# First attention of a four-part block on one core: TensorE turns x itself, the norm enters as scalars of the rows, and GpSimd splits one weight pair

## The reference, cut to what matters

```python
x = x + tanh(g_xattn[0]) * xattn0(layernorm(x), ctx)   # energy = (ctx Wq + bq)(ctx Wk + bk)^T; softmax; LN(x) @ att^T
x = x + tanh(g_ffn[0])   * ffn0(layernorm(x))          # ternary weights, rows rounded to 8 bits, SiLU gate
x = x + tanh(g_xattn[1]) * xattn1(layernorm(x), ctx)   # 16 heads, q and k RMS-normed, softmax, Wo
x = x + tanh(g_ffn[1])   * moe(layernorm(x))           # 64 experts, top 8, and a shared one
```

## Time and profile before

| | |
|---|---|
| time, median of 3 runs | 615.57 us (615.5 to 616.37) |
| span of the profiled execution | 614.4 us |
| TensorE busy | 604.4 us (98%) |
| VectorE busy | 477.4 us (78%) |
| ScalarE busy | 422.5 us (69%) |
| GpSimd busy | 235.1 us (38%) |

### The profile page before, as it was taken

The page is one execution under the profiler, slowest core; times in us unless marked ns, Lnnn a source line. Parts: engine busy times, 40 slices in busy tenths (PEclk is TensorE's granted clock), DMA queues, the critical chain, the costliest instruction groups (busy, mean ns, idle before and its releaser), DMA issues.

```text
span 614.4 us, 11617 instructions
## 1 busy us (share of the span) xinstructions
PE 604.4 (98%) x3644; PEld 525.1 (85%) x3644; DVE 477.4 (78%) x1139; ACT 422.5 (69%) x1082; POOL 235.1 (38%) x280
## 2 busy tenths in 40 slices
PE   8989999999999999999999999999999999999997
PEld 6757899999999999999998888888887888887886
DVE  3999988887777787688876787788777676777776
ACT  6999999888888888889897344465444444443442
POOL 5899998576665566656662020000000000000000
PEclk9999999999999999999999999999999999999999
DMA  8513302000000000000030544353856466555640
GB/s 294 201 53 102 92 13 78 2 2 2 2 1 2 1 2 2 1 2 1 11 121 2 169 150 152 128 171 97 215 156 167 116 174 175 153 158 152 188 133 34
DMA packets 33653, 56.47 MB, mean 92 GB/s; under 512 B 12800, under 2 KB 13504, under 8 KB 33600
## 3 DMA queue, kind: packets, MB, share of 16 engines
q1 hardware_dynamic: 33312, 55.82, 30.5%
q10 hardware_dynamic: 288, 0.00, 0.0%
HBM read 53.45 MB, written 1.31 MB: 89 GB/s over the span
## 4 chain that ended last, share of the span: by engine, by line
PE 87%; DVE 5%; ACT 3%; POOL 2%; issue 2%; DVEq 0%; POOLq 0%; ACTq 0%
PE bank L299 25%; PE bank L301 24%; PE bank L300 24%; PE bank L968 4%; PE bank L943 2%; PE bank L935 2%; DVE hs L2072 1%; PE bank L895 1%; PE bank L1009 1%; PE bank L815 1%; PE bank L821 1%; PE bank L888 1%; ACT w L1461 1%; PE bank L801 1%; POOL att L585 1%
## 5 line engine op out<-in xcount | busy, mean ns | idle before, releaser
L1607 ACT ACTIVATE inter_hi<-inter 128x512 fp32r<-128x512 f32 x63 | 39.8, 632 | 140.6 <-DVE inter L2271 140.6
L299 PE MATMUL bank<-xnT_hi,front_hi 128*128 128x512 f32 (+1 forms) x260 | 102.0, 392 | 0.0
L301 PE MATMUL bank<-xnT_hi,front_lo 128*128 128x512 f32 (+1 forms) x260 | 101.7, 391 | 0.0
L300 PE MATMUL bank<-xnT_lo,front_hi 128*128 128x512 f32 (+1 forms) x260 | 101.7, 391 | 0.0
L2275 DVE TENSOR_TENSOR inter_lo<-inter,inter_hi 128x512 fp32r<-128x512 f32 x63 | 43.6, 692 | 37.9 <-ACT inter_hi L1607 37.3
L1559 ACT ACTIVATE att<-bank,shift,rq 128x256 f32<-128x256 f32 x128 | 71.2, 572 | 0.0
L585 POOL TENSOR_TENSOR att<-att,rowinv 128x512 f32<-128x512 f32 x60 | 63.1, 1067 | 11.7 <-DVE rowinv L2171 11.7
L2244 DVE TENSOR_TENSOR prod<-gate_s,bank 128x512 f32<-128x512 f32 x63 | 43.2, 686 | 21.7 <-PE bank L301 19.6
L2154 DVE TENSOR_REDUCE rowmax<-bank 128x2 f32<-128x512 f32 x64 | 43.6, 685 | 21.0 <-PE bank L301 20.7
L300 PEld LDWEIGHTS bank<-xnT_lo,front_hi 128*128 128x128 f32 x260 | 48.9, 188 | 11.3
L301 PEld LDWEIGHTS bank<-xnT_hi,front_lo 128*128 128x128 f32 x260 | 48.8, 188 | 11.3
(11 more groups left out here) (271 smaller groups left out, 1813.1 us busy)
## 6 DMA issues: line engine op xcount, KB each, us to landing
w_all<-w_rows SPq DMA_DIRECT2D x128, 128.0 KB, 3.0
raw<-in_expert_w SPq DMA_DIRECT2D x32, 384.0 KB, 3.5
wvo_raw<-in_expert_w SPq DMA_DIRECT2D x16, 384.0 KB, 3.6
e_more<-in_expert_w SPq DMA_DIRECT2D x16, 384.0 KB, 3.6
raw<-in_head_qk SPq DMA_DIRECT2D x8, 384.0 KB, 3.2
wvo_raw<-in_head_vo SPq DMA_DIRECT2D x4, 384.0 KB, 3.8
w_keep<-in_head_vo SPq DMA_DIRECT2D x4, 384.0 KB, 3.6
gate_raw<-in_gate_wT SPq DMA_DIRECT2D x2, 704.0 KB, 8.8
```

The source lines that it names most:

```text
L299: pe.matmul(out, l_hi, r_hi_, start=start, stop=False, skip_group_check=True)
L300: pe.matmul(out, l_hi, r_lo_, start=False, stop=False, skip_group_check=True)
L301: return pe.matmul(out, l_lo, r_hi_, start=False, stop=stop, skip_group_check=True)
L1607: act.activation(inter_hi[:, slot, :], inter[:, slot, :], ACT.Copy).then_inc(a_Ihi, 1)
```

## The change

- The rows are no longer normed ahead of the first attention. `normalise_0` goes (eight calls), and `turn_rows_0` turns x as soon as it is loaded. Two of its calls stand earlier in TensorE's order, and one copy earlier in ScalarE's.
- `power_0` makes two more columns: `tg_rstd`, gate times r, and `tg_mean`, gate times r times m. `add_A` uses `tg_rstd` as its factor, one instruction for each tile. `tg_mean` is taken off in `add_output`, after the second attention, again one instruction for each tile.
- Pair 0's two parts are made by GpSimd (`both_w(0)`); `split_w(0)` and `low_w(0)` go. SP's wait for `load_qk(2)` and the counts of the other waits follow; `split_done(p)` on TensorE waits for `g_Wlo` at p = 0.

```diff
+        tg_rstd = sb("tg_rstd", [P, TILES])
+        tg_mean = sb("tg_mean", [P, TILES])
...
@@ SP's queue @@
             load_vo(2)
+            sp.wait_ge(g_Wlo, 1)
+            load_qk(2)
             sp.wait_ge(v_Wlo, 1)
-            load_qk(2)
-            sp.wait_ge(v_Wlo, 2)
             load_qk(3)
...
@@ GpSimd @@
+            def pool_high_w(p):
+
+                pool.wait_ge(l_hqk[p % 2], (p // 2) * 16 + 16)
+                pool.tensor_scalar(w_hi(p), raw[:, p % 2, :], 1.0, 0.0, ALU.mult, ALU.add).then_inc(g_Whi, 1)
+
+            def pool_low_w(p):
+                pool.wait_ge(g_Whi, 1 if p == 0 else 2)
+                pool.tensor_tensor(w_lo(p), raw[:, p % 2, :], f(w_hi(p)), ALU.subtract).then_inc(g_Wlo, 1)
+
             def both_w(p):
...
+                pool_high_w(p)
+                pool_low_w(p)
...
             def root_0(b):
                 c = slice(2 * b, 2 * b + 2)
                 pool.wait_ge(v_pw1, b + 1)
-                pool.tensor_scalar(negm[:, c], mv[:, c, 0], -1.0, 0.0, ALU.mult, ALU.add)
                 pool.tensor_scalar(vare[:, c], mv[:, c, 1], 1.0, EPS, ALU.mult, ALU.add).then_inc(g_va0, 1)
 
             def power_0(b):
...
-                pool.tensor_tensor(rstd[:, c], vare[:, c], minus_half[:, 0:2], ALU.pow).then_inc(g_pw1, 1)
+                link_g(pool, pool.tensor_tensor(rstd[:, c], vare[:, c], minus_half[:, 0:2], ALU.pow))
+                if b == 0:
+                    pool.wait_ge(a_tg, 1)
+                link_g(pool, pool.tensor_scalar(tg_rstd[:, c], rstd[:, c], tg[:, 0:1], 0.0, ALU.mult, ALU.add))
+                pool.tensor_tensor(tg_mean[:, c], mv[:, c, 0], tg_rstd[:, c], ALU.mult).then_inc(g_pw1, 1)
...
             root_0(0)
             power_0(0)
-            normalise_0(0)
-            normalise_0(1)
             root_0(1)
             power_0(1)
-            normalise_0(2)
-            normalise_0(3)
+            scale_gain(g1, l_g1)
             root_0(2)
             power_0(2)
-            normalise_0(4)
-            normalise_0(5)
-            scale_gain(g1, l_g1)
             root_0(3)
...
             scale_back_1(0)
             limit_1(0)
-            normalise_0(6)
+            both_w(0)
             scale_back_1(1)
+            limit_1(1)
             scale_gain(g2, l_g2)
-            normalise_0(7)
-            limit_1(1)
             times_gain(0)
...
@@ TensorE @@
             def turn_rows_0(b, bk):
 
-                pe.wait_ge(g_u0, 2 * b + 2)
+                pe.wait_ge(l_x[b // 2], 16)
                 for k in range(KH):
                     for t in range(2):
                         mm = pe.transpose(bank4(bk)[:, k, t * P:(t + 1) * P],
-                                          u[:, 2 * b + t, k * P:(k + 1) * P], ident[:, :])
+                                          x[:, 2 * b + t, k * P:(k + 1) * P], ident[:, :])
                 mm.then_inc(t_u0, 1)
...
             query_key(0, 2, 3)
             energy(0, 2)
+            turn_rows_0(0, 1)
             query_key(1, 2, 0)
             energy(1, 6)
             energy(2, 0)
-            turn_rows_0(0, 1)
             pe.wait_ge(a_eA, 4)
             turn_att(0, 6)
             energy(3, 3)
             mix(0, 1)
+            turn_rows_0(1, 5)
             turn_att(1, 2)
-            turn_rows_0(1, 5)
             sum_abs([0, 1], 0)
...
@@ ScalarE @@
             copy_qk(0, 2, 4, 3)
+            copy_rows_0(0, 1)
             copy_qk(1, 2, 5, 0)
             exp_A(0, 2)
             exp_A(1, 6)
-            copy_rows_0(0, 1)
...
             abs_down()
-            split_w(0)
             turn_gate(0)
...
@@ VectorE @@
             def add_A(b, bk):
                 dve.wait_ge(t_oA, b + 1)
-                if b == 0:
-                    dve.wait_ge(a_tg, 1)
-                xb = x[:, 2 * b:2 * b + 2, :]
-                dve.scalar_tensor_tensor(xb, bank4(bk), tg[:, 0:1], xb, ALU.mult, ALU.add).then_inc(v_xA, 1)
+                dve.wait_ge(g_pw1, b + 1)
+                for t in range(2):
+                    i = 2 * b + t
+                    ins = dve.scalar_tensor_tensor(x[:, i, :], bank4(bk)[:, t, :], tg_rstd[:, i:i + 1], x[:, i, :],
+                                                   ALU.mult, ALU.add)
+                ins.then_inc(v_xA, 1)
...
             def add_output(b):
 
                 dve.wait_ge(t_Y, 16 * b + 16)
-                xb = x[:, 2 * b:2 * b + 2, :]
-                dve.tensor_tensor(xb, bank4(YBK), xb, ALU.add).then_inc(v_Y, 1)
+                for t in range(2):
+                    i = 2 * b + t
+                    ins = dve.scalar_tensor_tensor(x[:, i, :], bank4(YBK)[:, t, :], tg_mean[:, i:i + 1], x[:, i, :],
+                                                   ALU.subtract, ALU.add)
+                ins.then_inc(v_Y, 1)
...
             absmax_1(1)
-            low_w(0)
             inv_max_1(1)
```

More of the change, by code:

```diff
@@ L159, in flamingo_kernel @@
         g_gain, v_sc1, v_sc2, g_sc1, g_sc2 = (sem(n) for n in ("g_gain", "v_sc1", "v_sc2", "g_sc1", "g_sc2"))
-        g_u0, t_u0, a_x0 = sem("g_u0"), sem("t_u0"), sem("a_x0")
+        t_u0, a_x0 = sem("t_u0"), sem("a_x0")
         g_u1, v_u, t_u, a_u, c_u = sem("g_u1"), sem("v_u"), sem("t_u"), sem("a_u"), sem("c_u")
@@ L237, in flamingo_kernel @@
                              "v_mq", "v_Olo", "v_Mlo", "v_gk"))
-        g_rk, g_rq, g_kn, g_att, v_Wlo, g_Wlo = (sem(n) for n in ("g_rk", "g_rq", "g_kn", "g_att", "v_Wlo", "g_Wlo"))
+        g_rk, g_rq, g_kn, g_att, v_Wlo, g_Wlo, g_Whi = (sem(n) for n in ("g_rk", "g_rq", "g_kn", "g_att", "v_Wlo", "g_Wlo",
+                                                                  "g_Whi"))
         dctx = ExitStack()
@@ L339, in _ @@
             load_vo(4)
-            sp.wait_ge(v_Wlo, 3)
+            sp.wait_ge(v_Wlo, 2)
             load_qk(4)
@@ L344, in _ @@
             load_vo(7)
+            sp.wait_ge(v_Wlo, 3)
+            load_qk(5)
             sp.wait_ge(v_Wlo, 4)
-            load_qk(5)
-            sp.wait_ge(v_Wlo, 5)
             load_qk(6)
-            sp.wait_ge(g_Wlo, 1)
+            sp.wait_ge(g_Wlo, 2)
             load_qk(PAIRS - 1)
             for q in range(2):
-                sp.wait_ge(g_Wlo, 4 + 3 * q)
+                sp.wait_ge(g_Wlo, 5 + 3 * q)
                 sp.dma_start(e_raw(q), expert_w[q]).then_inc(l_exp[q], 16)
@@ L447, in power @@
                 pool.tensor_tensor(dst, src, minus_half[:, 0:n], ALU.pow).then_inc(done, 1)
+            def pool_high_w(p):
[4 more added lines that the diff above has]
+                pool.tensor_tensor(w_lo(p), raw[:, p % 2, :], f(w_hi(p)), ALU.subtract).then_inc(g_Wlo, 1)
             def both_w(p):
-                pool.wait_ge(l_hqk[p % 2], (p // 2) * 16 + 16)
-                link_g(pool, pool.tensor_scalar(w_hi(p), raw[:, p % 2, :], 1.0, 0.0, ALU.mult, ALU.add))
-                pool.tensor_tensor(w_lo(p), raw[:, p % 2, :], f(w_hi(p)), ALU.subtract).then_inc(g_Wlo, 1)
+                pool_high_w(p)
+                pool_low_w(p)
             def low_w(p, piece):
                 c = slice(piece * 2 * P, (piece + 1) * 2 * P)
-                pool.wait_ge(a_Whi, p)
+                pool.wait_ge(a_Whi, p - 1)
                 pool.tensor_tensor(w_lo(p)[:, c], raw[:, p % 2, c], f(w_hi(p)[:, c]),
@@ L538, in limit_2 @@
                                    ALU.mult).then_inc(g_sc2, 1)
[L540 to L544, removed]
             def normalise_1(i):
@@ L901, in project, with split_done @@
                                 w_lo(p)[:, w0:w0 + 256], k == 0, last)
+            def split_done(p):
+                if p == 0:
+                    pe.wait_ge(g_Wlo, 1)
+                elif p < EARLY:
+                    pe.wait_ge(v_Wlo, p)
+                else:
+                    pe.wait_ge(g_Wlo, 3 * (p - EARLY) + 2)
             def proj_q(n, bk=QBK, fresh=False):
@@ L906, in proj_q @@
                 if b == 0:
-                    pe.wait_ge(*((v_Wlo, p + 1) if p < EARLY else (g_Wlo, 3 * (p - EARLY) + 1)))
+                    split_done(p)
                 if p == 0:
@@ L2063, in low_w @@
             def low_w(p):
-                dve.wait_ge(a_Whi, p + 1)
+                dve.wait_ge(a_Whi, p)
                 dve.tensor_tensor(w_lo(p), raw[:, p % 2, :], f(w_hi(p)), ALU.subtract).then_inc(v_Wlo, 1)
```

## The result

The changed kernel takes 619.09 us (619.01 to 619.39), the kernel before on the same chip 615.65 (615.5 to 616.37): ratio 1.0057, 95% interval 1.0045 to 1.007. It is slower by 3.4 us. I had forecast 616.6, with 617.6 as the upper end of the range: the sign of the likeliest case was right, its size three times too small. The profiled execution took 619.08, its span is 617.3, the granted clock 1.00 throughout. (One of the nine executions of the kernel before timed beside e9 to e11 took 970.47 at a mean granted clock of 0.571; it is left out of the ratios.)

A forecast was written before the change was run, and what follows sets the result against it. VectorE near 30 us was taken to set when TensorE's dense stretch begins, one for one. The front's delays and the GpSimd meetings summed to +1.05: span 614.4 to 615.45, time 616.6, range 614.9 to 617.6.

The forecast's parts named there:

- the likeliest case: The forecast itself, chance 0.50: the change makes the kernel slower, span +1.05 us, time 616.6.
- A halved `add_A`: VectorE's `add_A` as two 128x256 instructions instead of one 128x512: +0.11 us for each of four.
- `add_output` at 0: Cutting `add_output` in two, four times, costs 0, since TensorE is dense there and VectorE waits for it.
- What the two passes meet: GpSimd's high and low passes block VectorE for whole instructions, delaying `round_down` and `round_1(2)`; sum 0.84 to 1.25, taken 1.05.
- +0.13 forecast at `times_up_0(0)`: The late `turn_gate(0)` passes +0.13 down ScalarE's order to `silu_0(0)`, so VectorE's `times_up_0(0)` comes at 28.57.
- Either may be first: 0 or about +0.4: VectorE's `round_1(3)` and GpSimd's gain g2 meet near 30.9 us; delay 0 or about +0.4, tie left open.
- Start: x turned early: Four transposes of `turn_rows_0(0)` move onto TensorE's chain behind `energy(0)`, +0.44; `mix(0)` and `add_A(0)` inherit +0.36.
- GpSimd becomes the bound: Rival, chance 0.18: `round_down` precedes the high pass, `times_gain(0)` and normalised rows come late; +1.5 to +1.9, 617.3.
- The front alone: Rival, chance 0.20: only the late front costs, 0.35, small passes slip between GpSimd's passes; 615.9.
- the gain: Rival, chance 0.12: ScalarE's chain loses two copies, -1.2 if TensorE's 0.44 is absorbed; 614.4.
- `add_A(0)` before 17.2: Deciding sign for the rival of a shorter ScalarE chain; the forecast expected `add_A(0)` near 17.8.
- 1.2 us lie around the span: Profiled span 614.4 against the 615.57 median of three runs; used to turn span 615.45 into time 616.6.

The follow-up runs named there:

- e9: The changed kernel with GpSimd's low pass of pair 0 moved behind `times_gain(0)`, its high pass kept behind `limit_1(0)`: 619.44 us, ratio 1.0058.
- e11: As e10, and `times_gain(0)` on GpSimd also waits for `round_1(3)`: 620.48 us, ratio 1.0089.
- e2: As e1, with `turn_rows_0(0)` and its copy put back to their old places: 617.43 us, ratio 1.0025.
- e1: The changed kernel with pair 0's split given back to ScalarE and VectorE, x still turned raw, `add_A` still in two pieces: 618.01 us, ratio 1.0034.
- e6: As e2, with one more wait on GpSimd: `times_gain(0)` starts only when `round_1(3)` is done: 616.71 us, ratio 1.0007.
- e7: The changed kernel with GpSimd's low pass for pair 0 waiting until `scales_1(1)` is done: 617.8 us, ratio 1.0031.
- e3: The changed kernel with GpSimd's low pass for pair 0 cut into six instructions of 128 columns: 619.52 us, ratio 1.0053.
- e4: The changed kernel with GpSimd's `both_w(0)` moved ahead, behind `scale_gain(g1)`, and `root_0(3)`, `power_0(3)` moved behind `limit_1(0)`: 619.52 us, ratio 1.0056.
- e10: As e9, with `turn_rows_0(0)` and its copy at their old places: 618.22 us, ratio 1.0047.

## Why the prediction was wrong

**Right.** TensorE's dense stretch passes VectorE's delay on, one for one: +3.42 at `scales_1(2)`, 3.4 in the medians. The transposes stand on the chain with 0.44; `add_A(0)` is at +0.43 net of the later start, +0.36 forecast, and e2 against e1 gives 0.5 to 0.58. A halved `add_A` costs 0.12 to 0.14 from start to start of its neighbours (+0.11 forecast). `turn_gate(0)` and `silu_0(0)` did not become the bound in after, though VectorE waited for `silu_0(0)` in e1, e2, e6 and e7, and `low_w(0)` gave no gain by itself: `round_down`, meeting the high pass, used it up. The passes exclude each other as whole instructions: `scales_1(1)` took 1.76 beside the whole pass, 0.40 beside six pieces (e3). From `low_w(1)` on (1.55, 1.54 before) later meetings fell as before. `round_1(2)` lost 0.56, and 0.49 was forecast (0.62 with the 0.13 ahead of it), but by luck: g2 held it and not the low pass, since both were later.

**Nearly right: `add_output` at 0.** In the stretch where it runs, 143 to 316 us, after loses 0.19, e1 0.27, e6 0.27 and e7 0.27, and before nothing. That is common to all kernels with the x part, small, and not placed more closely.

**The step that failed is "What the two passes meet".** I listed what VectorE issues under the low pass as `round_down`, then `round_1(2)`, and left out `scales_1(1)`, which stands between them: 128x2 numbers, 0.14 us, below everything that I priced. Both its inputs are tensors in SBUF. It waits out the pass, and `times_up_0(0)` behind it in VectorE's order goes with it: +0.13 forecast at `times_up_0(0)`, +1.75 net of the start found. e7 took that meeting away and got 1.3 back. The Trainium skill, SBUF — State Buffer, "Who interferes with whom", has the rule in a form that covers it: it asks for two SBUF inputs, not for a size. The trace agrees: 1.76 for 128x2 numbers beside the pass, 0.14 without. I had cited it and applied it only to the large rows.

**The second miss is the "Either may be first: 0 or about +0.4" for `round_1(3)`.** It came out at 0.79, and against `times_gain(0)`, not g2. It is not due to the weights: e1 and e2 have it too, since the x part takes two normalisations from ahead of `times_gain(0)`. e6 shows it, worth 0.7.

**A third term was put at nothing: the second moved call.** "Start: x turned early" prices only `turn_rows_0(0)`. `turn_rows_0(1)` ahead of `turn_att(1)` makes `copy_att(1)` 0.34 later in e2.

So of the 3.4 us the x part holds 2.1 (e1). In its traces that is 0.5 to 0.6 for the first moved call, some 0.36 for the second, 0.7 to 0.8 for the freed GpSimd at `round_1(3)`, 0.16 at `round_1(2)`, 0.12 for the half of `add_A(2)` and 0.26 behind 143 us. The weights add 1.3: they cost 1.3 at `scales_1(1)` (e7) and 0.3 at `round_down`, more at `round_1(2)`, and give back the 0.86 of `low_w(0)`.

**The rivals.** "GpSimd becomes the bound" named a price closer to the result (617.3) for the wrong reason: GpSimd idles 1.91 at 34.75, and GpSimd late is nowhere on the chain behind 33 us. The front alone (615.9) and the gain (614.4) are excluded. Its sign, `add_A(0)` before 17.2, did appear (17.05), only because the first trace of before began slowly: a mark in absolute times can't be read across executions that differ by 1 us at the start. The same goes for the "1.2 us lie around the span": where one execution has both numbers, 1.8 lie between them (619.08 and 617.3; 615.19 and 613.4). The forecast isn't hurt, since 616.6 is the median and the 1.05.

**Open.** Where the last 0.2 us between 540 and 608 in after (also in e1 and e7, not in e6) come from. And whether any place for the passes pays: cutting the low pass (e3) or moving it (e4, e9 to e11) lost as much elsewhere, gating it (e7) gave 1.3 back, and no variant beat the kernel before.

## What to carry to other kernels

When work moves to GpSimd beside a full VectorE, list every instruction that VectorE issues under the new pass, the tiny ones first, and give each the rest of the pass if it reads two SBUF tensors or is a `tensor_scalar` from SBUF to SBUF like `round_1` and `round_down` here; what stands behind it in VectorE's order is late as well. Taking work from GpSimd is subject to the same list, because its next pass arrives earlier: here one added wait on GpSimd gave 0.7 us back. Before a pass is moved later, look up its first reader on TensorE, since a hole of 2.07 us there was followed by half the clock in most executions of e9 and e10. When several calls are moved ahead, price each one: the cost of the second showed on another engine, ScalarE.

## What the runs showed that I had not expected

- A 128x2 VectorE instruction took 1.764 us behind a GpSimd pass, 0.14 without it.
- TensorE's granted clock fell to 0.50 in the profiled executions of e3, e4, e9, e10 and e11, in each behind idle time that after and before don't have there (1.78 us in e3, 1.60 and 0.41 in e4, 2.07 in e9 and e10, 3.45 in e11), 0.3 to 2 us after work had resumed, and stayed there for 3 to 7 us. It did not fall in the trace of after, whose longest wait from 24 to 45 us is 0.97.
- Executions of one kernel differ by 1 us from line 815 on (592 or 379 ns for the same products), with a granted clock of 1.00 in both. The profiled executions of e7 (592) and e9 (573) began slowly too. The cause is open.
